# A vision block on one core: ScalarE's order of evicting edges and normalising rows, and where the last rows are scaled

## The chip, the cores and the metric

The kernel runs on one core of one Trainium2 chip. The metric is the device time of one execution in microseconds (us); lower is better. PE is TensorE, PEld its weight loads, DVE is VectorE, ACT is ScalarE, POOL is GpSimd, and SP is the sync engine, whose queue only issues DMAs here. Each engine works through its own list of instructions in order; a wait on a semaphore holds everything behind it on that engine.

## What is computed

Eight pictures of 3x256x256 go through one block: an edge filter, causal attention, a layer norm, a mixture of eight experts with a capacity of 320 tokens each, and a second layer norm. Cut to what matters:

```python
gray = einsum('bchw,c->bhw', x, (0.2989, 0.587, 0.114))
h = abs(conv3x3(gray, scharr_x, scharr_y)).sum(axis=1) / 2        # 8 x 256 tokens of 256
h = layernorm(h + softmax_causal((h Wq' + bq)(h Wk' + bk)' / 16) (h Wv' + bv))
t = h.reshape(2048, 256)
probs = softmax(t @ Wr)                                            # 8 experts
idx, pmax = argmax(probs), max(probs)
pos = place of the token among those of its expert, in order of tokens
kept = pos < 320
eout = relu(ein @ W1[e]) @ W2[e]                                   # ein: the kept tokens of expert e
out = where(kept, eout * pmax, t)
h = layernorm(h + out)
```

A token that is not kept adds itself, so its result is only its own row scaled once more; the kernel calls such a row `lone` and computes it for every token, later overwriting the kept ones.

## The kernel before

**Rounds.** The first part has a round `i` for each picture, 0 to 7 (`B` is 8, `L` is 7). In round `i` PE projects keys (`project_keys`, L1245) and values (L1157 to L1159) of picture `i`, makes its scores (L1282), counts the experts' tokens of picture `i-1` (`count`, L1310 to L1314), filters picture `i+1` (`convolve`, L1229: half `c` = 0 into PSUM bank 0, then half 1 into bank 1), transposes the probabilities (`prob_t`, L1292 to L1294), attends (L1298 to L1300) and transposes the tokens of picture `i+1` (`tokens_as_rows`, L1256). Products are made of high and low halves in fp32r, three matmuls for one.

ACT evicts and computes beside it. The steps that matter here: `edges(i+1, c)` (L604) writes the absolute value of bank `c` to `edges_abs`, a part of `tokens_mem`. When both halves are there, DVE adds them (`tokens`, L879, into `xT`), and PE's `tokens_as_rows` and ACT's `tokens_high` (L611) wait for that sum. `prob_t` (L652) copies the transposed probabilities, `norm_rows(i-1)` (L660) writes the normalised rows of the picture before to `trow`, `route_exp(i-1)` (L680) makes the exponentials of its routing softmax, `norm_lone(i-2)` (L669) writes the `lone` rows of the picture before that, and `gray_high` (L593) rounds a grey picture.

POOL computes the reciprocal roots (`scale_rows`, L461 and L462, into `rstd` and `nmr`; `scale_lone`, L473 to L478, into `lone_scale`) and writes rows to their experts' places in DRAM (`scatter`, L507, two indirect DMAs each, into `dispatched`). DVE makes the statistics (`moments`), the routing (`route`), the factor (`factor`, L985) and the slots (`assign`), and the low halves of the experts' weights (`split_low`, L891), whose high halves ACT makes (`split_high`, L691).

**The SP queue.** In step `i` of its loop SP loads a picture or weights, then stores the `lone` rows of picture `i-2` (`store_lone`, L344), and in step 7 behind that the 320 rows of expert 0 as far as they are known (`load_rows(0)`, L349 and L352, from `dispatched` into `images`). Then it stores the `lone` rows of the last two pictures, waits for all scatters (L391), loads the rows of all experts, and then weights.

**Between the parts.** The rows of pictures 6 and 7 are put into expert 0's transposed input by matmuls with 0/1 matrices: PE runs `place(6)` (L1360), `count(7)`, `early_turn` (L1370, which transposes the loaded rows into the same banks and waits for `load_rows(0)`), then `place(7)`, which waits for `norm_rows(7)`. ACT and DVE take the result out in high and low halves (`ein_t(0)`, L749 and L1078), and the first expert's matmuls start. `keep_warm(n)` (L1319) is n matmuls of 128x128 by 128x512 whose result nobody reads.

**Experts.** For each of the eight experts PE makes eight tiles of the hidden layer (`hidden(e, j)`) and adds each to the result two tiles later (`expert_out`). Each hidden tile goes through ACT (`h_hi`, L756), then DVE (`h_lo`, L1086), in two banks in turn; at j = 5 the next expert's rows are transposed (L1384).

What the two last `lone` writes stand between on ACT is four lines:

```python
            norm_lone(L - 1)
            norm_rows(L)
            route_exp(L)
            norm_lone(L)
```

## Time and profile before

| what | value |
|---|---|
| median of 3 runs | 271.15 us (270.98 to 271.69) |
| the profiled execution's own time | 271.74 us |
| its span, first to last instruction | 270.0 us |
| busy: PE, PEld | 242.4 us (90%), 227.4 us (84%) |
| busy: DVE, ACT, POOL | 181.1 us (67%), 153.4 us (57%), 95.0 us (35%) |
| mean granted clock of TensorE | 0.975 of full speed |
| rounds | seven starts of `project_keys`, 12.75 us apart from the second on |
| experts | about 15.93 us each, PE busy throughout |

A row of a timeline reads: start, duration, engine, line of the code, operation, out<-in, and, in brackets, how long the engine stood idle before it and what ended that. A count x2 says that several instructions are merged. The list of waits gives for each pair the total of idle time, how often, and the longest. Idle time of one engine costs nothing unless the engine that sets the end waits for it in turn, so PE's idle rows are read first and then followed back.

### The profile page before, as it was taken

The page shows a single profiled execution, that of the slowest core. Times are in us where ns is not written, and L with a number is a line of the kernel's source. Part 1 is how long each engine was busy: PE and PEld are TensorE (multiplying, and loading weights), DVE is VectorE, ACT ScalarE, POOL GpSimd, SP SyncE. Part 2 cuts the span into 40 slices and gives each one's busy share as a digit, 9 for nine tenths or more (in the row PEclk, how much of TensorE's full clock was granted, in tenths as well). Part 3 has the DMA queues.
Part 4 walks back from the last instruction along what each step waited for, and adds up shares of the span by engine and source line. Part 5 has one row for each costly group of instructions (what it writes and reads, how often), then busy time and mean ns, then how long its engine had stood idle before and what let it go on. Part 6 is the DMA issues. An engine that isn't in the chain of part 4 may idle for free.

```text
span 270.0 us, 5003 instructions
## 1 busy us (share of the span) xinstructions
PE 242.4 (90%) x1689; PEld 227.4 (84%) x1689; DVE 181.1 (67%) x546; ACT 153.4 (57%) x350; POOL 95.0 (35%) x172
## 2 busy tenths in 40 slices
PE   6999998988989898783899999999999999999940
PEld 5999897978979797662899999999999999999930
DVE  4864577676858596882655676796767779677530
ACT  4334556666667665744465547577575766756410
POOL 6001134646454544538100002425132252504473
PEclk9999999999999999999599999999999999999995
DMA  6856644182891110120689632708145180100000
GB/s 217 255 148 182 206 110 118 43 300 54 287 374 60 59 48 29 67 88 21 194 220 339 222 103 70 291 1 298 47 169 193 30 311 4 39 4 21 10 23 4
DMA packets 28122, 35.48 MB, mean 131 GB/s; under 512 B 2652, under 2 KB 24907, under 8 KB 28098
## 3 DMA queue, kind: packets, MB, share of 16 engines
q1 hardware_dynamic: 26016, 31.71, 36.7%
q0 software_dynamic: 1792, 3.47, 3.6%
q8 instruction: 13, 0.21, 0.3%
q14 instruction: 11, 0.09, 0.1%
q10 hardware_dynamic: 290, 0.00, 0.1%
HBM read 26.97 MB, written 9.47 MB: 135 GB/s over the span
## 4 chain that ended last, share of the span: by engine, by line
PE 78%; ACT 7%; DVE 5%; issue 5%; POOL 4%; POOLq 1%; DMA 0%; ACTq 0%; DVEq 0%
PE bank L1157 16%; PE bank L1159 15%; PE bank L1158 15%; PE bank L1229 11%; PE bank L1245 5%; PE bank L1282 4%; PE bank L1384 3%; ACT tokens_mem L604 2%; DVE xT L879 2%; PE bank L1256 2%; ACT trow L660 2%; PE bank L1435 2%; PE bank L1319 2%; POOL out_dram L547 1%; POOL dispatched L507 1%
## 5 line engine op out<-in xcount | busy, mean ns | idle before, releaser
L756 ACT ACTIVATE h_hi<-bank 128x320 fp32r<-128x320 f32 x58 | 25.4, 437 | 42.3 <-PE bank L1159 42.3
L1086 DVE SCALAR_TENSOR_TENSOR h_lo<-bank,h_hi 128x320 fp32r<-128x320 f32 x58 | 28.4, 489 | 30.5 <-ACT h_hi L756 27.7
L1157 PE MATMUL bank<-einT_hi,w_hi 128*128 128x320 f32 x128 | 41.4, 324 | 5.2 <-DVE einT_lo L1078 5.2
L1158 PE MATMUL bank<-einT_lo,w_hi 128*128 128x320 f32 x128 | 40.4, 315 | 0.0
L1159 PE MATMUL bank<-einT_hi,w_lo 128*128 128x320 f32 x128 | 40.4, 315 | 0.0
L891 DVE TENSOR_TENSOR w_lo<-w_raw,w_hi 128x1024 fp32r<-128x1024 f32 x32 | 38.9, 1214 | 0.0
L547 POOL DMA_INDIRECT out_dram<-tokens_mem,images x24 | 27.4, 1143 | 28.4 <-ACT tokens_mem L773 22.2
L1157 PE MATMUL bank<-h_hi,w_hi 128*128 128x320 f32 x112 | 35.4, 316 | 0.0
L1158 PE MATMUL bank<-h_lo,w_hi 128*128 128x320 f32 x112 | 34.6, 309 | 0.0
L1159 PE MATMUL bank<-h_hi,w_lo 128*128 128x320 f32 x112 | 34.6, 309 | 0.0
L691 ACT ACTIVATE w_hi<-w_raw 128x1024 fp32r<-128x1024 f32 x32 | 33.7, 1054 | 0.0
L1157 PEld LDWEIGHTS bank<-einT_hi,w_hi 128*128 128x128 f32 x128 | 24.9, 194 | 5.7 <-issue 5.6
L541 POOL TENSOR_TENSOR yrstd<-yve,minus_half 128x3 f32<-128x3 f32 x7 | 6.2, 884 | 66.4 <-DVE yve L1116 66.4
L1158 PEld LDWEIGHTS bank<-einT_lo,w_hi 128*128 128x128 f32 x128 | 24.9, 195 | 0.0
L1159 PEld LDWEIGHTS bank<-einT_hi,w_lo 128*128 128x128 f32 x128 | 24.8, 194 | 0.0
L1157 PEld LDWEIGHTS bank<-h_hi,w_hi 128*128 128x128 f32 x112 | 21.0, 188 | 0.5
L1158 PEld LDWEIGHTS bank<-h_lo,w_hi 128*128 128x128 f32 x112 | 21.1, 188 | 0.0
L1159 PEld LDWEIGHTS bank<-h_hi,w_lo 128*128 128x128 f32 x112 | 21.1, 188 | 0.0
L507 POOL DMA_INDIRECT dispatched<-trow,slot x16 | 17.3, 1084 | 7.1 <-issue 6.4
L879 DVE TENSOR_TENSOR xT<-tokens_mem 128x512 f32<-128x512 f32 x8 | 5.6, 699 | 17.5 <-ACT tokens_mem L604 17.5
L1229 PE MATMUL bank<-w_hi 128*128 128x260 f32 x96 | 14.9, 291 | 0.0
L1229 PE MATMUL bank<-w_lo,w_hi 128*128 128x260 f32 x96 | 14.9, 291 | 0.0
(210 smaller groups left out, 583.4 us busy)
## 6 DMA issues: line engine op xcount, KB each, us to landing
w_raw<-in_L_ffn_W_dram SPq DMA_DIRECT2D x16, 1024.0 KB, 7.9
images<-in_x_dram SPq DMA_DIRECT2D x7, 768.0 KB, 5.0
dispatched<-blank SPq DMA_DIRECT2D x4, 645.0 KB, 8.3
images<-dispatched SPq DMA_DIRECT2D x9, 258.0 KB, 3.4
out_dram<-lone SPq DMA_DIRECT2D x8, 256.0 KB, 3.7
images<-in_x_dram SPq DMA_DIRECT2D x2, 384.0 KB, 4.5
images<-dispatched SPq DMA_DIRECT2D x9, 64.5 KB, 3.8
out_dram<-tokens_mem,images POOLq DMA_INDIRECT x24, 3.5
```

The lines of the kernel that those rows point to most:

```text
L507: pool.indirect_dma_start(dispatched, bass.IndirectOffsetOnAxis(ap=slot[:, b % TR, s:s + 1], axis=0), trow[:, b % TR, s, :], None, bounds_ ...
L547: pool.indirect_dma_start(out_rows, bass.IndirectOffsetOnAxis(ap=ein[0:n, e, j, D + 1:D + 2].bitcast(U32), axis=0), z[0:n, e % 2, j, :], N ...
L691: act.activation(w_hi[:, e % 2, c], w_raw[:, e % 2, c], ACT.Copy).then_inc(w_hi_ready, 1)
L756: act.activation(hidden_halves(n)[0], bank[n % 2][:, 0:CAP], ACT.Relu).then_inc(h_hi_ready, 1)
L879: dve.tensor_tensor(xT[:, b % 2], edges_abs[:, :, 0, :], edges_abs[:, :, 1, :], ALU.add).then_inc(xT_ready, 1)
L891: dve.tensor_tensor(w_lo[:, e % 2, c], w_raw[:, e % 2, c], w_hi[:, e % 2, c].bitcast(F32), ALU.subtract).then_inc(w_lo_ready, 1)
L1086: dve.scalar_tensor_tensor(lo, bank[n % 2][:, 0:CAP], 0.0, hi.bitcast(F32), ALU.max, ALU.subtract).then_inc(h_ready, 1)
L1157: pe.matmul(to, ah, bh, start=first, stop=False)
L1158: pe.matmul(to, ah, bl, start=False, stop=False)
L1159: return pe.matmul(to, al, bh, start=False, stop=last)
L1229: ins = pe.matmul(acc[:, :, s * (S - REACH):s * (S - REACH) + REACH], half[:, b % 2, s, c * P + dx:c * P + dx + P], of_band[:, dx, :, 2 - ...
L1245: ins = pe.matmul(bank[3][:, c * S:(c + 1) * S], half[:, k, c * P:(c + 1) * P], of_x[:, b % 2, k, :], start=(t == c == k == 0), stop=(t == ...
```

## The change

Five things are altered.

1. In a round ACT evicts edge half 0 before the copy of the probabilities and half 1 right after it; `route_exp` comes next, then `tokens_high`, and `norm_rows` last. `route_exp` gets a wait on `rstd_ready`, and POOL's `scatter` one on `t_ready`.
2. The `lone` rows of picture 5 leave round 7: ACT writes them, and those of picture 6, after `norm_rows(6)`. The third piece of expert 0's weights is split next, before `norm_rows(7)`.
3. The `lone` rows of picture 7 are written inside expert 0, behind the second hidden tile, and stored by SP behind the loads of all experts' rows; POOL does both last scatters before it scales them.
4. On DVE `factor(6)` moves ahead of `route(7)`, and the low halves of pieces 1 and 2 stand around `factor(7)`.
5. PE gets 11 more `keep_warm` matmuls: 7 in place of 5 before `prob_t(7)`, 2 behind it, 3 before `place(7)`, 4 behind it.

```diff
@@ sync @@
-                if i >= 2:
+                if 2 <= i < B + 1:
                     store_lone(i - 2)
                 if i == L:
...
                 load_rows(e)
+            store_lone(L)
             for e in range(2, E):
@@ gpsimd @@
             def scatter(b):
                 pool.wait_ge(slot_ready, b + 1)
+                pool.wait_ge(t_ready, SC * (b + 1))
...
             scale_rows(L)
             scatter(L - 1)
+            scatter(L)
             scale_lone(L)
-            scatter(L)
@@ scalar @@
             def route_exp(b):
+                act.wait_ge(rstd_ready, b + 1)
...
-                if i >= 2:
+                if 2 <= i < L:
                     norm_lone(i - 2)
                 probs(i)
-                prob_t(i)
                 if i < L:
                     edges(i + 1, 0)
-                if i >= 1:
-                    norm_rows(i - 1)
+                prob_t(i)
                 if i < L:
                     edges(i + 1, 1)
                 if i >= 1:
                     route_exp(i - 1)
                 if i < L:
                     tokens_high(i + 1)
+                if i >= 1:
+                    norm_rows(i - 1)
+            norm_lone(L - 2)
             norm_lone(L - 1)
+            split_high(2)
             norm_rows(L)
             route_exp(L)
-            norm_lone(L)
-            split_high(2)
...
                     if j == 0:
                         split_high(4 * e + 3)
+                    if e == 0 and j == 1:
+                        norm_lone(L)
@@ vector @@
             residual(L)
+            factor(L - 1)
             route(L)
             moments(L)
-            factor(L - 1)
             assign(L)
+            split_low(1)
             factor(L)
-            split_low(1)
+            split_low(2)
...
-                    if j in (0, 1):
+                    if j in (0, 1) and 4 * e + j > 0:
                         split_low(4 * e + 2 + j)
@@ tensor @@
-            keep_warm(5)
+            keep_warm(7)
             prob_t(L)
+            keep_warm(2)
             attend(L)
...
             early_turn()
+            keep_warm(3)
             place(L)
+            keep_warm(4)
```

On ACT, in each of the rounds 1 to 6, here round 6. `tokens_mem<-bank` is an edge half, `trow` the normalised rows, `lexp` the routing exponentials, `w_hi<-xT` the high half of the tokens. Before:

```order
L644 ACTIVATE prob,psumr<-tokens_mem,nbias 128x256
L652 ACTIVATE probT<-bank 128x384
L604 ACTIVATE tokens_mem<-bank 128x512
L660 ACTIVATE trow<-resid,nmr,rstd 128x256 x2
L604 ACTIVATE tokens_mem<-bank 128x512
L680 ACTIVATE lexp,lsum<-lsub,rstd 128x8 x2
L611 ACTIVATE w_hi<-xT 128x512
```

After:

```order
L646 ACTIVATE prob,psumr<-tokens_mem,nbias 128x256
L606 ACTIVATE tokens_mem<-bank 128x512
L654 ACTIVATE probT<-bank 128x384
L606 ACTIVATE tokens_mem<-bank 128x512
L683 ACTIVATE lexp,lsum<-lsub,rstd 128x8 x2
L613 ACTIVATE w_hi<-xT 128x512
L662 ACTIVATE trow<-resid,nmr,rstd 128x256 x2
```

The two normalisations went from between the edge halves to the end of the round.

On ACT, from the copy of the last probabilities to the first hidden tile. `lone` are the lone rows of one picture (x2, a half each), `w_hi<-w_raw` a piece of weights, `einT_hi` expert 0's input. Before:

```order
L652 ACTIVATE probT<-bank 128x384
L660 ACTIVATE trow<-resid,nmr,rstd 128x256 x2
L680 ACTIVATE lexp,lsum<-lsub,rstd 128x8 x2
L669 ACTIVATE lone<-trow,lone_scale 128x256 x2
L660 ACTIVATE trow<-resid,nmr,rstd 128x256 x2
L680 ACTIVATE lexp,lsum<-lsub,rstd 128x8 x2
L669 ACTIVATE lone<-trow,lone_scale 128x256 x2
L691 ACTIVATE w_hi<-w_raw 128x1024
L749 ACTIVATE einT_hi<-bank 128x320 x2
L756 ACTIVATE h_hi<-bank 128x320
```

After:

```order
L654 ACTIVATE probT<-bank 128x384
L683 ACTIVATE lexp,lsum<-lsub,rstd 128x8 x2
L662 ACTIVATE trow<-resid,nmr,rstd 128x256 x2
L671 ACTIVATE lone<-trow,lone_scale 128x256 x4
L694 ACTIVATE w_hi<-w_raw 128x1024
L662 ACTIVATE trow<-resid,nmr,rstd 128x256 x2
L683 ACTIVATE lexp,lsum<-lsub,rstd 128x8 x2
L752 ACTIVATE einT_hi<-bank 128x320 x2
L759 ACTIVATE h_hi<-bank 128x320
L694 ACTIVATE w_hi<-w_raw 128x1024
L759 ACTIVATE h_hi<-bank 128x320
L671 ACTIVATE lone<-trow,lone_scale 128x256 x2
```

Nothing stands between the last `lexp` and `einT_hi` any more; the lone rows of picture 5 (the first two of the x4) come after the probabilities, and those of picture 7 after two hidden tiles.

On POOL, from the last `scale_rows` on (`rstd`, `nmr`); a `dispatched` row of x2 is one picture's scatter. Before:

```order
L461 TENSOR_TENSOR rstd<-ve,minus_half 128x2
L462 TENSOR_TENSOR nmr<-nmean,rstd 128x2
L507 DMA dispatched<-trow,slot 2560x258 x2
L473 TENSOR_TENSOR v<-rstd 128x2
L474 TENSOR_TENSOR v2n<-v,mv 128x2
L475 TENSOR_SCALAR v2e<-v2n 128x2
L478 TENSOR_TENSOR lone_scale<-v2e,minus_half 128x2
L507 DMA dispatched<-trow,slot 2560x258 x2
```

After:

```order
L462 TENSOR_TENSOR rstd<-ve,minus_half 128x2
L463 TENSOR_TENSOR nmr<-nmean,rstd 128x2
L509 DMA dispatched<-trow,slot 2560x258 x4
L474 TENSOR_TENSOR v<-rstd 128x2
L475 TENSOR_TENSOR v2n<-v,mv 128x2
L476 TENSOR_SCALAR v2e<-v2n 128x2
L479 TENSOR_TENSOR lone_scale<-v2e,minus_half 128x2
```

The last picture's scatter went ahead of the four steps that give `lone_scale`.

## Rows read from the trace of the kernel before

**Rows 1.** Waits between 30 and 110 us: total us, times, longest.

```profile
PE bank L1256 <- DVE xT L879: 6.5, 6, 1.1
```

**Rows 2.** Timeline of ACT, end of round 4: start, us, then as in the text.

```profile
64.66 0.49 ACT L652 ACTIVATE probT<-bank 128x384 f32<-128x384 f32 x1 [2.32 <-PE bank L1294]
65.05 0.59 ACT L604 ACTIVATE tokens_mem<-bank 128x512 f32<-128x512 f32 x1
65.52 1.09 ACT L660 ACTIVATE trow<-resid,nmr,rstd 128x256 f32<-128x256 f32 x2
66.51 0.59 ACT L604 ACTIVATE tokens_mem<-bank 128x512 f32<-128x512 f32 x1
...
67.46 0.20 ACT L680 ACTIVATION_READ_ACCUMULATOR lexp<-lsub,rstd 128x1 f32 x1
67.86 0.63 ACT L611 ACTIVATE w_hi<-xT 128x512 fp32r<-128x512 f32 x1 [0.20 <-DVE xT L879]
...
70.28 0.84 ACT L618 ACTIVATE w_hi<-bank,key_bias 128x256 fp32r<-128x256 f32 x2 [1.27 <-PE bank L1245]
```

**Rows 3.** Timeline of PE, the same stretch.

```profile
64.38 0.98 PE L1229 MATMUL bank<-w_lo,w_hi 128*128 128x260 f32 x6
...
66.20 0.61 PE L1300 MATMUL bank<-val,probT 128*128 128x264 f32 x2
67.88 0.66 PE L1256 MATMUL bank<-ident,xT 128*128 128x128 f32 x4 [1.07 <-DVE xT L879]
```

**Rows 4.** Timeline of SP in round 7, and its row loads' us from issue to landing.

```profile
112.78 0.37 SPq L344 DMA_DIRECT2D out_dram<-lone  x1
...
114.16 0.50 SPq L352 DMA_DIRECT2D images<-dispatched  x1
...
DMA to landing us min/median/max: 2.6/2.7/2.8
```

**Rows 5.** Timeline of ACT from the last probabilities to expert 0.

```profile
114.81 1.09 ACT L660 ACTIVATE trow<-resid,nmr,rstd 128x256 f32<-128x256 f32 x2
...
120.99 1.09 ACT L660 ACTIVATE trow<-resid,nmr,rstd 128x256 f32<-128x256 f32 x2 [3.72 <-POOL nmr L462]
...
126.44 0.91 ACT L669 ACTIVATE lone<-trow,lone_scale 128x256 f32<-128x256 f32 x2 [3.79 <-POOL lone_scale L478]
...
128.20 0.74 ACT L749 ACTIVATE einT_hi<-bank 128x320 fp32r<-128x320 f32 x2
```

**Rows 6.** Timeline of PE, the same stretch and the first expert's start.

```profile
111.35 1.38 PE L1319 MATMUL bank<-w_hi 128*128 128x512 f32 x5
...
118.82 2.06 PE L1370 MATMUL bank<-ident,images 128*128 128x128 f32 x12
121.74 2.39 PE L1360 MATMUL bank<-sums,trow 128*128 128x320 f32 x8 [0.86 <-ACT trow L660]
129.28 0.60 PE L1157 MATMUL bank<-einT_hi,w_hi 128*128 128x320 f32 x1 [5.16 <-DVE einT_lo L1078]
...
134.02 0.31 PE L1157 MATMUL bank<-h_hi,w_hi 128*128 128x320 f32 x1
```

**Rows 7.** One stretch of 1 us: busy of PE, PEld, DVE, ACT, POOL; granted clock; DMA share; GB/s.

```profile
127.00:128.00 1.00, 0.00 (x0) 0.00 (x0) 0.00 (x0) 1.00 (x2) 0.70 (x2) 0.50 0.04 8
```

**Rows 8.** Timelines of DVE and POOL at the last scatters.

```profile
122.77 1.20 DVE L891 TENSOR_TENSOR w_lo<-w_raw,w_hi 128x1024 fp32r<-128x1024 f32 x1
...
123.01 1.81 POOL L507 DMA_INDIRECT dispatched<-trow,slot  x1 [0.30 <-issue]
...
127.97 0.97 POOL L507 DMA_INDIRECT dispatched<-trow,slot  x1 [0.30 <-issue]
```

**Rows 9.** Expert 2's weights: the issue on SP, us to landing, first use on ACT.

```profile
141.13 0.47 SPq L339 DMA_DIRECT2D w_raw<-in_L_ffn_W_dram  x1
...
DMA to landing us min/median/max: 5.0/6.7/8.4
...
152.25 1.05 ACT L691 ACTIVATE w_hi<-w_raw 128x1024 fp32r<-128x1024 f32 x1
```

## The prediction

> **What bounds the kernel now.** I read the list of waits for PE first, since PE is busy for 90% of the span and nothing else comes near it. In the rounds it has one repeated wait: six times about 1.07 us for DVE's sum `xT` [rows 1]. The timelines of ACT and PE show what lies behind it [rows 2, 3]. DVE's sum needs both edge halves, and ACT writes the second at 66.51, although the filter on PE (start 64.38, 0.98 long) is done at 65.36. In between ACT runs the two normalisations of the picture before, from 65.52 to 66.51. So the wait is an order of ACT's own making. The second place is the gap between the two parts: PE stands idle for 5.16 us before the first expert [rows 6], because ACT reaches `einT_hi` only at 128.20, after the last `lone` rows, for which it waited 3.79 us on POOL's `lone_scale`, and a piece of weights [rows 5]. In that gap the granted clock falls to 0.50 [rows 7], the lower of the two levels (1.2 against 2.4 GHz), so the first expert starts at half speed. After that the experts run with PE busy throughout, and whatever is won before them should move their end rigidly.
>
> **1. The edge half, rounds 1 to 6.** Edge half 0 moves ahead of the copy of the probabilities. ACT stood idle for 2.32 us before that copy [rows 2], and filter half 0 is long done, so its 0.47 us (start to start, 65.05 to 65.52) cost nothing. Half 1 then starts when the filter is done, at 65.42 instead of 66.51. It ends 0.59 later at 66.01; from the end of an edge half to PE's transposes it took 66.51 + 0.59 = 67.10 to 67.88, that is 0.78 [rows 2, 3]. So the transposes can start at 66.79. The attention matmuls before them end at 66.81. 67.88 becomes 66.81: 1.07 us, the whole wait. What is late next? `tokens_high` needs the sum too and started at 67.86; it would start at 66.79. Ahead of it now stands only `route_exp`: from 66.98 (66.51 + 0.47) to 67.66, 0.68 long, so it runs from about 65.89 to 66.57 and is out of the way. Behind `tokens_high` now come the normalisations, 0.99 us start to start. ACT had 1.27 us idle before it evicts the next keys (70.28), and both ends of that stretch move together, so 0.28 us of cover is left. If that were short, the keys would be late by what is missing. Nobody needs `trow` before the next round's scatter, so the two added semaphore waits find their values there; behind POOL's stand only small operations, behind ACT's stands `tokens_high`. Bounds: 0 if something else takes the place of the wait, 6.5 (the total of the waits) if all of it goes. I take 6 x 1.07 = **6.4 us**, since each successor was followed and is covered. All later times are given on the clock of the old trace, as if the rounds had not moved.
>
> **2. The rows of expert 0.** The `lone` rows of picture 5 leave round 7, and this has a price that the code of ACT does not show. On SP `load_rows(0)` stands behind `store_lone(5)`. Before, that store went out at 112.78 and the second load at 114.16, landing at most 2.8 us later, at 116.96 [rows 4]; `early_turn` ran at 118.82 with no wait [rows 6]. Now ACT does, from 114.81 (when the normalisations could start [rows 5]): `route_exp` 0.68, `norm_rows(6)` 0.99, `norm_lone(5)` 0.91 [rows 5], ending at 117.39. The store goes out at 117.42, the second load about 0.84 later, behind a store and a load of 0.4 us each, at 118.26, and lands at 121.06 by the same 2.8. `early_turn` waits for it, as does POOL's `scatter(6)`. So PE runs from 121.06: `early_turn` 2.06, three `keep_warm` 0.83 (1.38 for five), `place(7)` 2.39, four `keep_warm` 1.10 [rows 6]. That is 6.38; each merged row holds the drain of its last matmul, which the next group covers. I take 0.25 for each of three, an estimate near the 0.31 of a single matmul, and get 126.7 (126.0 to 127.5 with 0.5 and 0 for the drains and 0.3 us for the landing). `norm_rows(7)`, at 120.99 before, and the picks of DVE are ready by then, so `place(7)` waits for nothing.
>
> **3. From place to the first expert.** `einT_hi` no longer waits for `lone_scale` or the weight piece. Before, from its start at 128.20 to PE's at 129.28 it took 1.08 [rows 5, 6] for the first half, and PE needs the second only after three matmuls. First-half work overlaps `place(7)`, and the second half fits under the four `keep_warm`. So the first expert starts at 126.7 instead of 129.28: **2.6 us**. Upper bound, if the rows came in time: `place(7)` at 121.74, 2.39 and 1.10 less two drains, 124.8 and 4.5 us. Lower bound 1.8.
>
> **4. The clock.** Before, 18 matmuls of the first hidden tiles ran from 129.28 to 134.02, 4.74 us, against 0.15 for each at full speed (an expert of 15.93 us holds 96 of them beside 1.7 us of transposes), so 2.65, and about 0.2 for the wait on ACT and DVE that comes up when tiles are short. That gives **1.9 us** if the clock stays up. What speaks for it: the gap of step 2, from the end of `count` at about 118.8 to 121.06, is 2.3 us, and the 5.16 us gap had the clock fall some 3 us after PE's last matmul; a gap of 0.86 left it alone [rows 6, 7]. Between them nothing is shown.
>
> **5. The lone rows of picture 7 and the scatters.** ACT comes to them after two hidden tiles, some 2.75 us behind the start, at 129.4. POOL must have `lone_scale` by then, now behind four scatter DMAs in place of two. One ran 1.81 while DVE split weights (122.77 for 1.20 [rows 8]), against 0.97 undisturbed. Both splits now fall on `scatter(6)`: from 121.1 with starts 1.3 apart and 1.5 us of blocking for the two splits, the four end at about 127.8 to 128.4; then the steps to `lone_scale`, which took 124.82 to 126.44, 1.6: 129.4 to 130.0. ACT waits 0 to 0.6, writes for 0.91, and the third hidden tile's eviction starts at 130.9 at the latest. PE needs it for the fifth tile at about 132.1, so nothing is lost; with an earlier start of the expert it would be. The Trainium skill says why the DMA was long (SBUF — State Buffer, "Who interferes with whom"): a DVE instruction with two SBUF inputs contends with a GpSimd instruction that reads SBUF, and the later one blocks fully. By that rule `lone_scale` comes at the later time, without it 1.5 us sooner; the sum is the same by both.
>
> **6. Weights of expert 2.** Their loads stand behind all row loads, which wait for the last scatter (127.97 + 0.97 before, at about 128.4 now), and behind one more store. So they are issued at about 141.1 as before and land within 8.4, at 149.5 [rows 9]. ACT used them at 152.25 and now wants them 4.5 us sooner, at 147.7. It may be held for 1.8 us, and a hidden tile's eviction may be late by about 1.7 us before PE waits (three tiles of six matmuls, 0.88 each, less 0.95 for ACT and DVE). Price 0 to 1 us; I take 0, and 1 for the range. The other edits (`factor(6)` sooner by some 0.1 us, seven `keep_warm` before `prob_t(7)` and two behind) lie under waits that end later, and step 2 now sets the end there.
>
> **The sum.** 6.4 + 2.6 + 1.9 = 10.9 us. The profiled execution took 271.74, which gives 260.8; against the median of 271.15 it gives **260.3**, which is my forecast. A measurement of this kernel can tell about 0.3% (0.8 us) from no change.
>
> **Rivals.**
> - *The clock falls in the new gap.* PE idles for 2.3 us just before `early_turn`, after a stretch of tiny matmuls. At half speed 18 matmuls cost 4.74 instead of 2.65 [rows 6]; a low stretch of 4 to 7 us costs 2 to 3.4. Time 262.3 to 263.7. Against: that gap is under half of the one that did it. Chance 0.22.
> - *POOL and SP become the bound inside expert 0 and 1.* The scatters block longer than reckoned, `lone_scale` comes later, and ACT holds the third eviction; or expert 2's weights are late. Price 1 to 2 us, 261.3 to 262.3. For: both have under 1.2 us of cover. Chance 0.13.
> - *The rows of expert 0 come in time after all,* `place(7)` starts near 121.6 and the entry gains 4.5 in place of 2.6: 258.4. Against: the queue's order. Chance 0.08.
> - *`norm_rows` at the round's end runs over its 0.28 us of cover* and makes the keys late, say 0.3 us a round: 1.8 us, 262.1. Chance 0.05.
> - *Slower than before: the clock goes down at the gap and stays down.* Half speed costs 2.09 in each 4.74 us, 0.44 a microsecond. From 25 us on it outweighs the 10.9; over two experts, 32 us at half, it costs 14 and the time is 274. Against: in the trace the clock came back after some 4 us of work. Chance 0.02.
>
> **How the numbers follow.** Forecast 0.50, and the rivals 0.22, 0.13, 0.08, 0.05 and 0.02. The range reaches from the early rows at 258.4 to the middle of the clock case with its upper part, 263.2. It leaves out the last case and the far ends of two. All cases but the last are faster by more than 0.3%: faster 0.97, same 0.01 for a mixture of losses that I have not named, slower 0.02.
>
> **What would show it.** Step 1: PE's wait L1256 for `xT` is gone from rounds 1 to 6, rounds are 11.7 us apart, and ACT still has a short wait before it evicts the keys. Step 2: PE waits about 2.3 us before `early_turn` for the DMA into `images`; if there is no such wait, or `place(7)` is what waits, the step is wrong. Step 3: `einT_hi` follows `place(7)` within 0.1 us. Step 4: clock 1.00 from 110 us to the end of the experts, and hidden tiles at 0.15 a matmul at once. Step 5: ACT's wait on `lone_scale` under 1 us, and no wait of PE on `h_lo` in expert 0 over 0.3. The forecast fails most easily by the clock and by the landing time of that one load, on which everything up to the first expert now hangs.

## The result, and the profile after the change

The changed kernel took **263.73 us** (262.65 to 264.17), the kernel before beside it 271.42 us (270.98 to 272.11). The ratio is 0.970, with a 95% interval of 0.966 to 0.975: a gain of 3.0%. Five later runs gave 263.11 us. Forecast were 260.3 us, with a range of 258.4 to 263.2, so the first median lies above the range and the later one just inside it. The direction was right, and the gain was short by a good 3 us. Single executions can fall into a slower state; one run of `e8_pool_swap` and one of the kernel before did, and they are left out of every number here.

The profiled execution took 263.28 us against 271.74. To find where the time went I cut both executions at four marks that PE passes in every kernel: the first projection of keys of round 0, that of round 7, the first matmul of expert 0 (`einT_hi` or `einT_lo` as input), and its first matmul on `h_hi`. The last piece is what remains of the execution's own time, so the five add up to it.

| piece, us | before | after | gain | forecast |
|---|---|---|---|---|
| to the keys of round 0 | 18.73 | 18.78 | -0.05 | 0 |
| keys of round 0 to keys of round 7 | 88.04 | 81.98 | 6.06 | 6.4 |
| keys of round 7 to expert 0 | 22.51 | 21.73 | 0.78 | 2.6 |
| expert 0 to its first `h_hi` matmul | 4.74 | 3.08 | 1.66 | 1.9 |
| from there to the end | 137.72 | 137.71 | 0.01 | 0 |
| sum | 271.74 | 263.28 | 8.46 | 10.9 |

Three quarters of what is missing lies in one piece, the entry into the experts. Its timeline on PE answers to [rows 6]; the columns are start, duration, engine, line, operation, out<-in, shape, count, and the idle time before with what ended it.

```profile
110.12 2.39 PE L1367 MATMUL bank<-tokens_mem,trow 128*128 128x320 f32 x8
...
112.59 0.17 PE L1320 MATMUL bank<-onehot,tri 128*128 128x8 bf16 x1
115.01 2.26 PE L1377 MATMUL bank<-ident,images 128*128 128x128 f32 x12 [2.25 <-DMA images<-dispatched]
117.19 1.65 PE L1325 MATMUL bank<-w_hi 128*128 128x512 f32 x3
118.64 3.08 PE L1367 MATMUL bank<-sums,trow 128*128 128x320 f32 x8
121.31 1.33 PE L1325 MATMUL bank<-w_hi 128*128 128x512 f32 x4
122.49 0.31 PE L1163 MATMUL bank<-einT_hi,w_hi 128*128 128x320 f32 x1
...
125.57 0.31 PE L1163 MATMUL bank<-h_hi,w_hi 128*128 128x320 f32 x1
```

The 5.16 us of idle time before the first expert [rows 6] are gone. In their place stands 2.25 us before `early_turn` (L1377), for the DMA into `images`, the rows of expert 0. But `place(7)` (L1367) takes 3.08 us, where the same eight matmuls of `place(6)` take 2.39 just above, and three `keep_warm` (L1325) take 1.65. The stretches of 1 us say why; the columns are the length, PE's busy time and count, the granted clock, the DMA share and GB/s.

```profile
114.00:115.00 1.00, 0.00 (x0) 1.00 0.88 304
115.00:116.00 1.00, 0.99 (x6) 1.00 0.12 41
116.00:117.00 1.00, 1.00 (x7) 0.88 0.00 0
117.00:118.00 1.00, 1.00 (x4) 0.50 0.04 13
118.00:119.00 1.00, 1.00 (x3) 0.50 0.18 59
119.00:120.00 1.00, 1.00 (x3) 0.50 0.20 70
120.00:121.00 1.00, 1.00 (x4) 0.91 0.19 65
```

The granted clock was at 1.00 through the idle time and fell to 0.50, from 2.4 to 1.2 GHz, only while PE was at work again. By the shares of the stretches it fell at about 116.8 and was back at about 120.2, 3.4 us later. So the old half-speed stretch in the first expert [rows 7] has moved to where `place(7)` runs.

What was awaited is shown by the chain that ended last (start, us, what): ACT's last `lone` row of picture 5, its store on SP, then the loads that stand behind it.

```profile
110.78 0.50 ACT lone L671
111.29 0.37 SPq L344
111.79 0.39 SPq L349
112.22 2.74 DMA images<-dispatched
115.01 2.26 PE bank L1377 x12
```

In the rounds PE's wait for `xT` [rows 1] is gone. Round 4 on ACT answers to [rows 2]: edge half 1 (63.39) now starts 0.29 us after the copy of the probabilities and waits only for its bank, `tokens_high` follows the sum, and 0.28 us are left idle before the keys' eviction at 67.25, the cover that was worked out.

```profile
62.61 0.49 ACT L654 ACTIVATE probT<-bank 128x384 f32<-128x384 f32 x1 [1.15 <-PE bank L1300]
63.39 0.60 ACT L606 ACTIVATE tokens_mem<-bank 128x512 f32<-128x512 f32 x1 [0.29 <-PE bank L1235]
...
64.83 0.63 ACT L613 ACTIVATE w_hi<-xT 128x512 fp32r<-128x512 f32 x1 [0.28 <-DVE xT L884]
65.36 1.08 ACT L662 ACTIVATE trow<-resid,nmr,rstd 128x256 f32<-128x256 f32 x2
66.35 0.62 ACT L595 ACTIVATE w_hi<-red 128x512 fp32r<-128x512 f32 x1
67.25 0.84 ACT L620 ACTIVATE w_hi<-bank,key_bias 128x256 fp32r<-128x256 f32 x2 [0.28 <-PE bank L1251]
```

### The profile page after: what moved, and what is told of

It is laid out like the page before. It is cut to its first block, busy times and chain, and to the rows that moved or that the text cites. A ratio compares the mean times of both kernels' runs of the same rounds, so it can differ in the third digit from the quotient of the medians.

```text
span 261.5 us, 5032 instructions
## 1 busy us (share of the span) xinstructions
PE 244.8 (94%) x1700; PEld 228.4 (87%) x1700; DVE 181.6 (69%) x546; ACT 155.1 (59%) x350; POOL 96.8 (37%) x172
## 4 chain that ended last, share of the span: by engine, by line
PE 49%; POOL 2%; issue 2%; DMA 1%; ACT 1%; DVE 1%; POOLq 1%; SPq 0%; DVEq 0%
PE bank L1163 14%; PE bank L1165 14%; PE bank L1164 14%; PE bank L1393 3%; PE bank L1444 2%; POOL out_dram L549 1%; PE bank L1367 1%; DMA images<-dispatched 1%; PE bank L1325 1%; PE bank L1377 1%; POOL yrstd L572 1%; POOLq L67 1%; ACT trow L662 0%; ACT lone L671 0%; POOL ynmr L573 0%
## 5 line engine op out<-in xcount | busy, mean ns | idle before, releaser
L1163 PE MATMUL bank<-einT_hi,w_hi 128*128 128x320 f32 x128 | 40.4, 316 | 0.2 <-DVE h_lo L1092 0.2
L1165 PE MATMUL bank<-einT_hi,w_lo 128*128 128x320 f32 x128 | 39.6, 309 | 0.0
L1164 PE MATMUL bank<-einT_lo,w_hi 128*128 128x320 f32 x128 | 39.5, 309 | 0.0
L1163 PEld LDWEIGHTS bank<-einT_hi,w_hi 128*128 128x128 f32 x128 | 24.1, 188 | 0.6 <-DVE h_lo L1092 0.4
L1164 PEld LDWEIGHTS bank<-einT_lo,w_hi 128*128 128x128 f32 x128 | 24.1, 188 | 0.0
L1165 PEld LDWEIGHTS bank<-einT_hi,w_lo 128*128 128x128 f32 x128 | 24.0, 188 | 0.0
L606 ACT ACTIVATE tokens_mem<-bank 128x512 f32<-128x512 f32 x16 | 9.6, 598 | 9.2 <-PE bank L1235 9.2
```

The costliest lines, as they stand in the source:

```text
L606: act.activation(edges_abs[:, c].rearrange("p f s -> p (f s)"), bank[c][:, :], ACT.Abs).then_inc(edges_ready, 1)
L1163: pe.matmul(to, ah, bh, start=first, stop=False)
L1164: pe.matmul(to, ah, bl, start=False, stop=False)
L1165: return pe.matmul(to, al, bh, start=False, stop=last)
```

## The experiments

The theory after the result had three parts. **A**: the rounds gave what they promised but for about 0.09 us each; the clock's fall in the entry cost what the entry lacks; and its cause is PE's wait for the rows of expert 0, which SP loads late. The rivals: the entry is bound by DVE, POOL or ACT whatever the clock does; the added `keep_warm` are what costs; or the rows are late for another reason than SP's order. One table holds the pieces of each profiled execution, cut as above; the texts point to it.

| kernel | to keys 0 | rounds | entry | first tiles | rest | own time |
|---|---|---|---|---|---|---|
| before | 18.73 | 88.04 | 22.51 | 4.74 | 137.72 | 271.74 |
| after | 18.78 | 81.98 | 21.73 | 3.08 | 137.71 | 263.28 |
| e11_after_again | 18.83 | 81.90 | 21.71 | 3.09 | 137.79 | 263.32 |
| e1_rounds_only | 20.89 | 81.89 | 22.51 | 4.22 | 137.82 | 267.33 |
| e6_tail_only | 17.97 | 88.01 | 21.79 | 3.08 | 137.73 | 268.58 |
| e2_fill_gap | 18.31 | 81.88 | 20.10 | 3.08 | 137.74 | 261.11 |
| e4_no_warm | 18.32 | 82.00 | 20.34 | 3.73 | 137.72 | 262.11 |
| e7_before_filled | 18.96 | 87.98 | 22.53 | 3.39 | 137.80 | 270.66 |
| e3_rows_first | 17.96 | 81.94 | 17.94 | 3.09 | 139.00 | 259.93 |
| e5_lone_later | 18.80 | 81.97 | 17.94 | 3.08 | 137.75 | 259.54 |
| e8_pool_swap | 17.89 | 85.23 | 17.89 | 3.09 | 137.74 | 261.84 |
| e9_narrow_add | 18.64 | 81.60 | 17.94 | 3.08 | 138.30 | 259.56 |
| e12_narrow_weights | 18.23 | 81.59 | 17.93 | 3.08 | 137.75 | 258.58 |
| e13_later_weights | 18.80 | 81.96 | 17.89 | 3.08 | 137.75 | 259.48 |

The first column shows that the time up to the first keys differs by up to 3 us between executions, though up to there all these kernels run the same instructions in the same order (but for the narrow addition of two of them); the pieces behind it repeat to about 0.1 us where the code is the same. So pieces are compared first, and medians second. For the highest value, the 20.89 of `e1_rounds_only`, the trace shows most of the cause: the granted clock was at 0.50 for 3.4 us from about 12.2 on, with PE busy, while in the thirteen others it was at 1.00 there.

### The parts apart: e1_rounds_only and e6_tail_only

`e1_rounds_only` is the kernel before with part 1 of the change alone:

```diff
                 probs(i)
-                prob_t(i)
                 if i < L:
                     edges(i + 1, 0)
-                if i >= 1:
-                    norm_rows(i - 1)
+                prob_t(i)
...
                     tokens_high(i + 1)
+                if i >= 1:
+                    norm_rows(i - 1)
```

> The kernel before with only part 1 of the change: ACT's new order within a round, and the two semaphore waits that go with it. Theory (the rounds' gain is independent of the rest): rounds of 11.7 to 11.8 us, the start of the last keys 6.0 us earlier, the gap before the first expert unchanged at about 5.2 us with the clock falling to 0.50 in it, so 271.4 - 6.0 = 265.4 us. Rival (the gap between the parts gives part of it back, since POOL and SP come no sooner): 267 us or more, with a longer idle time of PE before the first expert.

It took 265.49 us (264.47 to 267.33), ratio 0.977 (0.973 to 0.981). The forecast of the sum held: a round is 11.77 us long and the rounds give 6.15 us. The entry is 22.51 us as before. Its profile holds a surprise. `place(7)` stands behind a gap of 0.87 us, as it did before [rows 6], and takes 4.08 us in place of 2.39 (timeline of PE):

```profile
114.83 2.06 PE L1372 MATMUL bank<-ident,images 128*128 128x128 f32 x12
117.75 4.08 PE L1362 MATMUL bank<-sums,trow 128*128 128x320 f32 x8 [0.87 <-ACT trow L661]
```

The stretches of 1 us of the same execution, with PE's busy time and the granted clock:

```profile
117.00:118.00 1.00, 0.25 (x1) 0.99 0.00 0
118.00:119.00 1.00, 1.00 (x3) 0.50 0.00 0
...
120.00:121.00 1.00, 1.00 (x4) 0.50 0.00 0
```

It cost nothing there, because ACT came to `einT_hi` only at 124.21 anyway, behind the last `lone` rows and a piece of weights. The clock came back, and fell once more in the gap before the first expert, so the first tiles took 4.22. But the prediction had argued from just this row of before that a gap of 0.86 leaves the clock alone. Up to `place(7)` PE's work and its waits in this piece are those of the kernel before to a hundredth of a microsecond (`early_turn` 12.05 us after the keys of round 7 in both), so the length of a gap does not decide alone.

`e6_tail_only` is the other half: the changed kernel with the old order of ACT in the rounds, that is, the diff above turned round.

> The changed kernel with ACT's old order within a round, so that only the parts between the rounds and the experts are changed. Theory A (the parts add up: 6.0 us for the rounds and 2.4 for the entry, of which 1.7 are the clock of the first tiles): rounds 12.75 us apart as before, a wait of about 2.3 us for expert 0's rows, the first expert about 0.8 us earlier than before and at full speed, 269.0 us. Theory B (the entry part alone gives nothing, since the late rows and the extra matmuls eat it): 271.4 us.

It took 268.52 us (267.53 to 269.16), ratio 0.986 (0.982 to 0.990). Its entry and first tiles are those of the changed kernel (21.79 and 3.08), the 2.31 us of wait before `early_turn` too. By the pieces, the rounds' gain in the one (6.15) and the gain of entry and first tiles in the other (2.38) make 8.53 us, and the same pieces of the changed kernel 8.50: the parts add up, and don't touch each other.

### The clock in the entry: e2_fill_gap, e4_no_warm and e7_before_filled

`e2_fill_gap` gives PE work that nobody reads while it waits:

```diff
             count(L)
+            keep_warm(10)
             early_turn()
```

> The changed kernel with ten more matmuls nobody reads on PE between the count of picture 7 and the turning of expert 0's rows, about 2.1 us in a gap of 2.25 us; nothing else moves. Theory A (the clock fell because of this gap, and that is the larger part of what the prediction missed): the clock stays at 1.00 from the rounds to the end of the experts, the three keep_warm take 0.7 instead of 1.5 us and place(7) 2.4 instead of 3.1, the first expert starts 1.7 us earlier, 262.0 us or less by the median, and the runs lie closer together than 262.65 to 264.17. Theory B (the late rows alone, the clock would have cost nothing on this path): 263.7 as the changed kernel.

It took 261.68 us (261.11 to 263.79), ratio 0.965 (0.961 to 0.970). Its timeline of PE has no gap, and `place(7)` takes 2.32 us:

```profile
112.05 2.53 PE L1325 MATMUL bank<-w_hi 128*128 128x512 f32 x10
114.41 2.06 PE L1377 MATMUL bank<-ident,images 128*128 128x128 f32 x12
116.40 0.97 PE L1325 MATMUL bank<-w_hi 128*128 128x512 f32 x3
117.20 2.32 PE L1367 MATMUL bank<-sums,trow 128*128 128x320 f32 x8
```

One of its stretches of 1 us, all of which from 112 to 119 show a granted clock of 1.00:

```profile
117.00:118.00 1.00, 1.00 (x5) 1.00 0.23 72
```

The data came no sooner (`early_turn` starts 14.22 us after the keys of round 7, 14.25 in the changed kernel), yet the entry went from 21.73 to 20.10. These **1.63 us are the price of the clock's fall**, measured with nothing else changed. It also shows that PE's own matmuls set the entry from `early_turn` on: had another engine been the bound, the entry would not have followed the clock. One part of the expectation failed, that the runs would lie closer together. Five of the six took 261.11 to 261.75, but one took 263.79, at a mean granted clock of 0.979 where the others had 0.986 to 0.988; it has no trace, so where its clock fell is not known.

`e4_no_warm` takes all 11 added `keep_warm` out:

```diff
-            keep_warm(7)
+            keep_warm(5)
             prob_t(L)
-            keep_warm(2)
...
-            keep_warm(3)
             place(L)
-            keep_warm(4)
```

> The changed kernel without its eleven added keep_warm matmuls. Theory A (with the rows late, the three before place(7) lie on the path and the clock falls anyway): the first expert starts 1.4 us earlier, 262.3 us. Theory B (they keep the clock from falling further or longer): a longer stretch at 0.50 and 264 us or more.

It took 262.31 us (262.05 to 263.16), ratio 0.967 (0.963 to 0.970). The first expert starts 1.39 us sooner, as expected, but its first tiles take 3.73 us with the clock at 1.00, partly since PE now waits 0.31 us for `einT_lo`. Entry and first tiles come to 24.07 us together, 24.81 with the fillers. `early_turn` starts at the same time after the keys (14.26 us, 14.25 in the changed kernel), so the four fillers around `prob_t(7)` change nothing. The seven around `place(7)` cost about 0.7 us in the changed kernel and kept no clock up: the low stretch lasted 3.4 us with them and without. They stand behind the gap, not in it.

`e7_before_filled` asks what the fall cost in the kernel before:

```diff
             place(L)
+            keep_warm(22)
```

> The kernel before with 22 more matmuls nobody reads behind place(7), about 4.7 us in the gap of 5.16 us. Nothing that is waited for moves. Theory A (the half clock in the first tiles is all that this gap costs beyond its length): the first expert starts as before, its first 18 matmuls take 3.1 instead of 4.7 us, 269.8 us. Theory B (the clock comes back by itself without a cost on the path): 271.4 us.

It took 270.25 us (269.63 to 270.77), ratio 0.994 (0.991 to 0.997). The first tiles took 3.39 us in place of 4.74, so the fall had cost 1.35 us there; 3.1 were expected. In the changed kernel and eight of its variants the same 18 matmuls take 3.08 or 3.09 us, not the 2.85 that the prediction had reckoned.

### The order on SP: e3_rows_first and e5_lone_later

`e3_rows_first` puts the rows of expert 0 ahead of the store that waits for ACT:

```diff
-                if 2 <= i < B + 1:
-                    store_lone(i - 2)
                 if i == L:
...
                     load_rows(0)
+                if 2 <= i < B + 1:
+                    store_lone(i - 2)
```

> The changed kernel with SP's load of expert 0's rows issued ahead of the store of picture 5's lone rows in round 7; ACT's order is untouched. Theory A (the load was late only because of the queue): it is issued about 4 us earlier, near 108, PE turns the rows right after the count at about 112.8 with no wait, place(7) waits for the last normalised rows and starts at about 115.5, the clock stays up, and the first expert starts near 119 instead of 122.5: 260 us. Theory B (POOL's last scatters and the lone rows of picture 7 then take the bound in the first expert): PE waits up to 1.7 us for the third hidden tile, 261 to 262 us.

It took 260.33 us (259.78 to 262.58), ratio 0.962 (0.957 to 0.967), near the 260 of theory A, with a part of theory B's loss in it. `early_turn` starts at 111.76 without a wait, the clock stays at 1.00 with no filler, and the entry is 17.94 us: 3.79 less than in the changed kernel, 1.63 of it the clock and 2.16 the rows. But 1.29 us were given back later (rest 139.00). The timeline of ACT in expert 0:

```profile
122.91 0.91 ACT L671 ACTIVATE lone<-trow,lone_scale 128x256 f32<-128x256 f32 x2 [2.27 <-POOL lone_scale L479]
```

That of POOL, with the first scatter DMA and the last step to `lone_scale`:

```profile
114.60 1.93 POOL L509 DMA_INDIRECT dispatched<-trow,slot  x1 [0.70 <-ACT trow L662]
...
121.22 1.65 POOL L479 TENSOR_TENSOR lone_scale<-v2e,minus_half 128x2 f32<-128x2 f32 x1
```

That of DVE, with the weight split beside it:

```profile
121.07 1.22 DVE L896 TENSOR_TENSOR w_lo<-w_raw,w_hi 128x1024 fp32r<-128x1024 f32 x1
```

And that of PE, where the wait ends up:

```profile
124.71 0.41 PE L1163 MATMUL bank<-einT_hi,w_hi 128*128 128x320 f32 x1 [0.98 <-DVE h_lo L1092]
```

With an earlier first expert ACT reaches the `lone` rows of picture 7 before POOL has their scale, waits 2.27 us, and holds the eviction of the next hidden tile. Step 5 of the prediction had said so: "with an earlier start of the expert it would be". POOL's last step took 1.65 us beside a weight split on DVE, where it took 0.72 in the changed kernel. `e5_lone_later` moves the `lone` rows on:

```diff
-                    if e == 0 and j == 1:
+                    if e == 0 and j == 6:
                         norm_lone(L)
```

> The kernel with the rows of expert 0 loaded first, and ACT's lone rows of picture 7 moved from behind the second to behind the seventh hidden tile of expert 0. Theory A (POOL's four scatters before lone_scale are what held ACT for 2.27 us and PE for about 1.2 us there): ACT does not wait for lone_scale, PE's waits for h_lo in expert 0 fall to 0.3 us or less, 259.3 us against 260.3. Theory B (the late row loads or weights hold PE next): same as 260.3, with a wait of PE on DMA or of ACT on w_raw in experts 0 or 1.

It took **259.75 us** (259.14 to 261.25), ratio 0.955 (0.951 to 0.959). The rest is back at 137.75 us. By the pieces it is 3.74 us better than the changed kernel, through two edits of a few lines.

### The missing 0.09 us a round: e8_pool_swap and e9_narrow_add

Rounds 1 and 6 of the changed kernel are 11.70 and 11.68 us long, those between 11.78; 11.70 was forecast. DVE's sum falls onto the end of POOL's addition of the blue share, here in the timeline of DVE, round 4:

```profile
64.02 0.77 DVE L884 TENSOR_TENSOR xT<-tokens_mem 128x512 f32<-128x512 f32 x1 [1.19 <-ACT tokens_mem L606]
```

And in that of POOL:

```profile
62.97 1.27 POOL L517 TENSOR_TENSOR red<-red,images 128x512 f32<-128x512 f32 x1 [1.23 <-DVE red L832]
```

`e8_pool_swap` (on top of `e5_lone_later`) was meant to part the two:

```diff
-                if i + 2 < B:
-                    add_blue(i + 2)
                 if i >= 1:
                     scale_lone(i - 1)
+                if i + 2 < B:
+                    add_blue(i + 2)
```

> The kernel of e5 with POOL's two pieces of work at the end of a round swapped: the four small steps to lone_scale first, then the addition of the blue part, 128x512. In the changed kernel DVE's sum of the edge halves starts while POOL's addition runs, and takes 0.77 us where it took 0.70 before. Theory A (that overlap of two operations that both read SBUF costs the 0.08 us by which most rounds are longer than 11.70): with the addition starting later, not sooner, than DVE's sum, the sum takes 0.69 us and rounds are 11.70 us, 0.4 us less by the end. Theory B (the overlap has nothing to do with it): rounds of 11.78 us as in e5, same time.

Neither expectation held: 263.10 us (261.84 to 265.07), ratio 0.971 (0.966 to 0.976), and rounds of 12.44 us. The addition had moved the wrong way, and the sum now starts inside it (timeline of DVE, then of POOL):

```profile
64.44 1.44 DVE L884 TENSOR_TENSOR xT<-tokens_mem 128x512 f32<-128x512 f32 x1 [1.18 <-ACT tokens_mem L606]
```

```profile
64.05 1.28 POOL L517 TENSOR_TENSOR red<-red,images 128x512 f32<-128x512 f32 x1
```

The sum ends at 65.88, which is 0.55 us after POOL's addition at 65.33, and alone it takes 0.69: it stood almost still meanwhile. The expectations missed where the addition would land; the mechanism itself shows more plainly, with 0.75 us on top in place of 0.08. `e9_narrow_add` cuts the addition from 1.27 to 0.22 us and leaves it in its place; most of the blue share is left out of the pictures:

```diff
-pool.tensor_tensor(red[:, b % 2], red[:, b % 2], pix[:, b % 2, 2], ALU.add)
+pool.tensor_tensor(red[:, b % 2, :, 0:8], red[:, b % 2, :, 0:8], pix[:, b % 2, 2, :, 0:8], ALU.add)
```

> This is e5_lone_later with POOL's addition of the blue share cut from 512 columns to 16 (8 of each half), so the grey pictures lack most of their blue; the instruction stays in its place. Theory A (DVE's sum and POOL's addition hinder each other when they overlap, which costs about 0.09 us a round): DVE's sum takes 0.69 us in every round as in the kernel before, in place of 0.69 to 0.82, and the rounds are 11.68 to 11.70 us long in place of 11.78; over six rounds 0.5 us, so about 259.2 us where e5_lone_later has 259.75. Theory B (the 0.09 us a round are drains and hand-overs that the prediction left out): the sum takes 0.69 but the rounds stay at 11.78, and the time stays at 259.75.

The pieces say A, at 0.37 us in place of the 0.5 expected. The sum takes 0.69 us in all rounds but one (0.73), and the seven rounds 81.60 us in place of 81.97; with that the rounds' gain over before is 6.44 us, the forecast's 6.4. The time did not show it: 259.49 us (258.41 to 261.08), ratio 0.957 (0.953 to 0.961), no different from `e5_lone_later`. The rest grew from 137.75 to 138.30, so another wait had taken the gain.

```profile
ACT w_hi L694 <- DMA w_raw<-in_L_ffn_W_dram: 3.1, 1, 3.1
...
PEld bank L1163 <- DVE w_lo L896: 0.3, 1, 0.3
```

These are two lines of its list of waits from 118 to 150 us (total, times, longest): expert 2's weights. Their loads were issued at 131.8 and 132.3, behind all row loads and a store, and ACT took the first at 142.64, after waiting 3.06 us. The first issue on SP and the first use on ACT, here:

```profile
131.77 0.47 SPq L335 DMA_DIRECT2D w_raw<-in_L_ffn_W_dram  x1
142.64 1.06 ACT L694 ACTIVATE w_hi<-w_raw 128x1024 fp32r<-128x1024 f32 x1 [3.06 <-DMA w_raw<-in_L_ffn_W_dram]
```

And in `e5_lone_later`, where PE lost nothing to them:

```profile
132.28 0.47 SPq L335 DMA_DIRECT2D w_raw<-in_L_ffn_W_dram  x1
142.35 1.06 ACT L694 ACTIVATE w_hi<-w_raw 128x1024 fp32r<-128x1024 f32 x1 [2.23 <-DMA w_raw<-in_L_ffn_W_dram]
```

The loads went out equally long after expert 0's start in both (13.59 and 13.57 us), so they move along with a sooner entry. What differs is the time from issue to use, 10.87 against 10.07 us; no run shows why.

### Expert 2's weights: e12_narrow_weights and e13_later_weights

Both move those loads ahead of the row loads of experts 3 to 7, on top of `e9_narrow_add` and of `e5_lone_later`:

```diff
                 load_rows(e)
+                if e == 2:
+                    load_first(2)
+                    load_second(2)
             store_lone(L)
-            for e in range(2, E):
+            for e in range(3, E):
```

> This is e9_narrow_add (blue share cut to 16 columns) with the loads of expert 2's weights moved on SP ahead of the row loads of experts 3 to 7. In e9_narrow_add the first expert started 0.53 us sooner than in e5_lone_later (118.18 against 118.71), and by expert 2 nothing of it was left (149.01 against 149.04); ACT waited 3.1 us for those weights. Theory A (the weights of expert 2 took the gain back): they are issued near 125 in place of 131.8, ACT's wait for them is under 0.5 us, expert 2 starts 0.5 to 0.7 us sooner (near 148.4), and the time is 0.5 us under that of e9_narrow_add, near 259.0. Theory B (something else in expert 1 or 2 holds PE, such as the high and low halves on ACT and DVE): ACT's wait goes, but expert 2 starts at 149.0 and the time stays at 259.5.

> This is e5_lone_later with the same move of expert 2's weight loads, and nothing left out. There PE lost at most 0.1 us to those weights, so theory A expects no difference that can be measured: 259.4 to 259.8 us, with ACT's wait of 2.2 us for the weights down to under 0.5 us. Theory B (other stages of expert 1 hold PE) expects the same time and leaves the rival without a gain in either kernel. A time over 260.5 would mean that the later row loads of experts 3 to 7 or the store of the lone rows behind them cost something.

`e12_narrow_weights` took 259.20 us (258.58 to 261.18), ratio 0.958 (0.953 to 0.962). The medians can't tell it from `e9_narrow_add`, but the pieces can: ACT's wait is gone and the rest is 137.75 us again, 0.55 less, as theory A said. `e13_later_weights` took 259.59 us (258.97 to 261.66), ratio 0.958 (0.953 to 0.963), the same as `e5_lone_later`, as expected. So these weights took the gain of `e9_narrow_add`, in the one execution of it that has a trace. In the changed kernel ACT does not wait for them, in `e5_lone_later` it waits 2.23 us and PE loses nothing, and 0.8 us more from issue to use cost PE about half a microsecond. Whether that longer load comes with the narrow addition or varies between executions stays open.

### The changed kernel once more: e11_after_again

> The changed kernel itself once more, beside the others. By its first four runs 263.7 us (262.65 to 264.17). Theory A (the clock falls in the wait for the rows of expert 0 in every execution): every run lies between 262.5 and 264.5 and the profile shows the granted clock at 0.50 for 3 to 4 us before the first expert. Theory B (it falls in some executions only, and the profiled one was such a case): some runs lie near 261.7, the time of e2_fill_gap, where the clock stayed up.

It took 263.11 us (262.59 to 263.84), ratio 0.970 (0.966 to 0.974), and its pieces are those of the first profile. Theory A holds as far as can be seen: none of its nine runs came near the 261.7 of the filled gap. The other profiles agree. All four with a wait of 2.2 to 2.3 us before `early_turn` (the changed kernel twice, `e6_tail_only`, `e4_no_warm`) show the clock at 0.50 for 3.4 us behind it; the seven variants of the changed kernel in which PE has no wait there (`e2`, `e3`, `e5`, `e8`, `e9`, `e12`, `e13`) show 1.00 throughout.

## Why the prediction was right, and where it failed

**Step 1, the edge half: right, and 0.34 us too large.** The wait is gone in each round, and the cover of 0.28 us came out to the digit. The sum 6 x 1.07 lacked one follower: with edge half 1 a microsecond earlier, DVE's sum starts inside POOL's addition and takes 0.77 in place of 0.69. `e9_narrow_add` shows that this is the difference. The Trainium skill states the rule (SBUF — State Buffer, "Who interferes with whom"): a DVE instruction with two SBUF inputs and a GpSimd instruction that reads SBUF exclude each other, the later one waiting in full. The traces agree but for a small remainder: in `e8_pool_swap` the sum overlaps the addition by 0.89 us and takes 0.75 longer, in round 4 of the changed kernel by 0.22 and takes 0.08 longer, both times the overlap less 0.14. The prediction had used this rule for the scatters and not for the instruction that it moved.

**Step 2, the rows of expert 0: the mechanism right to 0.04 us.** On the old clock (6.01 us later) the data was there at 121.02 against 121.06 forecast, after a gap of 2.25 against 2.3. What followed failed: `early_turn`, `place(7)` and seven `keep_warm` were to take 5.6 us and took 7.48 (115.01 to 122.49). With the clock up they take 5.88 (114.41 to 120.29 in `e2_fill_gap`), so about 0.25 us is the estimate of the drains, and 1.6 the clock.

**Step 3, the entry: its 2.6 us were 0.8.** Its own claim holds, that `einT_hi` follows `place(7)` without waiting for `lone_scale`; the time came from step 2.

**Step 4, the clock, is the step that failed.** "Clock 1.00 from 110 us to the end of the experts" did not come; the clock fell behind the wait before `early_turn`, which was the first rival, at a chance of 0.22 and with 262.3 to 263.7 us. The step argued from the length of gaps alone: 5.16 us had done it, 0.86 had not, and 2.3 was held to be harmless because it is under half of the long one, with nothing shown between. `e1_rounds_only` then showed a fall behind a gap of 0.87. The step was also drawn in the wrong place. It gave 1.9 us to the first tiles, and these 1.66 came, since the fall was over by then; the loss landed one stage earlier, on the matmuls of the entry. The rival's price, 2 to 3.4 us for a low stretch of 4 to 7 us in the hidden tiles, was too high: the stretch lasted 3.4 us and cost 1.63 (`e2_fill_gap`). That the measured time lies at the top of its 262.3 to 263.7 is luck, since 0.8 us of other losses and 1.0 us of compared runs fill it up.

**Step 5, the lone rows: the price of nothing was right, the times were not.** `lone_scale` was there at 122.81, 128.8 on the old clock and not at 129.4 to 130.0, and ACT, held back with the late expert, took it at 125.17 without waiting. Two weight splits were to block the scatters for 1.5 us; only one did, for 0.6: the first scatter DMA began 0.61 us before the end of a split and took 1.56 us in place of 0.97, and the second split ran while that DMA was already under way and in the pause behind it. So the cover was larger than reckoned. The remark that an earlier start would lose there was borne out by `e3_rows_first`, with 1.3 us.

**Step 6, expert 2's weights: price 0, right, but not tested at the times that were forecast.** The second load went out at 133.65, 139.7 on the old clock where 141.1 was assumed, and the first expert started 1.8 us later than forecast, so ACT did not wait at all. With the first expert 3.8 us sooner, in `e5_lone_later`, it waited 2.23 us and PE still lost nothing.

The sum by steps, in the profiled executions, of what is missing: 0.34 us from step 1, 1.82 from steps 2 and 3 (1.63 of it the clock), 0.24 from step 4 and 0.04 outside all steps, together 2.44 of 10.9. The other microsecond between 260.3 and 263.73 is a matter of which runs are compared: the profiled execution of before lay 0.59 above the median that the forecast was set against, and that of after 0.45 below its own.

The range was too tight at its upper end. It reached to the middle of the clock rival, the likeliest of all, and left out that this rival adds to the errors of the sum, which mostly go one way: a follower that was overlooked costs time and never gives any.

## What to carry to other kernels

When a step waits for data, list what each earlier move in the same change has put ahead of that data's load on the DMA queue: here a store that waited for ACT held two loads that had nothing to do with it, and two lines that swap them gave over a third of what the whole change gave. A gap of 2.25 us on PE cost twice here, once for itself and once for the half-speed stretch behind it, and the second price fell on what ran next; fill the gap itself, or better remove it, since fillers behind it cost their own time. And when an instruction is moved earlier, look at what the neighbour engines do at its new time, not only at what it no longer waits for.

## What the runs showed of the hardware

- In the changed kernel the granted clock fell about 4 us after PE's last work before the gap, when PE had already been busy again for nearly 2 us, and stayed at 0.50 for 3.4 us of full work. In the kernel before it fell 2.8 us into the gap of 5.16 us and was back 4.5 us after PE had begun again. In one execution (`e1_rounds_only`) it fell after a gap of 0.87 us, where the kernel before had stayed at 1.00 behind 0.86 with the same work ahead of it. What else decides it was not settled here.
- The price of a fall was 1.63 us in the entry (`e2_fill_gap`) and 1.35 us in the kernel before (`e7_before_filled`), by filling each gap.
- A DVE sum of 0.69 us took 1.44 when it began inside POOL's 1.28 us addition. A POOL step of 0.72 us took 1.65 beside a DVE split, and a scatter DMA 1.93 in place of 0.97 (both in `e3_rows_first`).
- From the first `h_hi` matmul to the end, twelve of the fourteen profiled executions took 137.71 to 137.82 us: that part follows its start rigidly. The time up to the first keys varied from 17.89 to 20.89 us; the highest value has a stretch of 3.4 us at a granted clock of 0.50, and the rest of the spread was not looked into.
